# Switched attention: output products for the chosen experts only, through slots in DRAM

## The reference

```python
gate = (one_hot(top2(sigmoid(raw))) * vals / vals.sum()).sum(-2)       # [B, S, H, E], two of eight not zero
q, k = per head x @ q_w[h].T, x @ k_w[h].T
xv = jnp.einsum('bsd,hedp->bshep', x, v_w.reshape(H, E, D, P))
v = jnp.einsum('bshep,bshe->bhsp', xv, gate_v)
att = softmax(jnp.einsum('bhqp,bhkp->bhqk', q, k) * SCALE)
ctx = jnp.einsum('bhqk,bhkp->bqhp', att, v)
weighted = ctx[:, :, :, None, :] * gate_o[..., None]
out = jnp.einsum('bshep,hepd->bsd', weighted, o_w.reshape(H, E, P, D))
```

## Time and profile before

| | us |
|---|---|
| median of 3 runs | 2651.47 (2650.15 to 2653.01) |
| profiled execution: time, span | 2653.63, 2651.9 |
| TensorE busy | 2339.9 (88%) |
| VectorE busy | 1732.3 (65%) |
| ScalarE busy | 1372.8 (52%) |
| GpSimd busy | 539.1 (20%) |
| mean granted clock of TensorE | 0.951 |

### The profile page before, as it was taken

One profiled execution on the slowest core, in us unless ns is written; L12 is line 12 of the kernel. 1 busy time (PEld: TensorE's weight loads), 2 busy tenths in 40 slices (PEclk: granted clock), 3 DMA queues, 4 the chain that ended last, 5 costly groups with the idle time before them and its releaser, 6 DMA issues. The chain is left out here.

```text
span 2651.9 us, 51036 instructions
## 1 busy us (share of the span) xinstructions
PE 2339.9 (88%) x15539; PEld 1826.2 (69%) x15539; DVE 1732.3 (65%) x4474; ACT 1372.8 (52%) x3690; POOL 539.1 (20%) x639
## 2 busy tenths in 40 slices
PE   7679999859999958888699999589999999999995
PEld 5457777748999845555477777477777777777762
DVE  2346766755888656666367667546676776767677
ACT  2146666744666525555276667465444444444430
POOL 3000000010111230000100000054343343434321
PEclk9789999969999979999799999789999999999998
DMA  2065566323666410000455665010010100101000
GB/s 79 0 153 121 120 119 129 74 69 93 217 207 212 126 50 1 0 0 0 105 133 120 121 131 118 23 52 17 21 37 2 36 17 22 36 1 37 1 1 28
DMA packets 182198, 187.58 MB, mean 71 GB/s; under 512 B 55281, under 2 KB 173506, under 8 KB 182018
## 3 DMA queue, kind: packets, MB, share of 16 engines
q1 hardware_dynamic: 178466, 176.18, 26.7%
q0 software_dynamic: 3552, 9.18, 1.2%
HBM read 144.23 MB, written 41.09 MB: 70 GB/s over the span
## 5 line engine op out<-in xcount | busy, mean ns | idle before, releaser
L800 ACT ACTIVATE cross_pr<-cross_sc,cross_mn 112x375 f32<-112x375 f32 x512 | 310.4, 606 | 233.0 <-DVE cross_mn L890 232.1
L2385 ACT ACTIVATE switch_vt<-switch_ps,switch_chosen 112x128 f32<-112x128 f32 x1024 | 290.3, 368 | 266.2 <-PE switch_ps L106 255.8
L890 DVE CUSTOM_DVE_ANT_0 cross_sc<-cross_ps,cross_masked 112x375 f32<-112x375 f32 x512 | 273.3, 544 | 178.4 <-PE cross_ps L688 157.5
L2459 DVE SCALAR_TENSOR_TENSOR all_x<-switch_ps,switch_go,all_x 112x256 f32<-112x256 f32 x512 | 245.7, 480 | 217.7 <-PE switch_ps L106 212.2
L696 PE MATMUL cross_ps<-all_ident,cross_pr 112*125 112x112 f32 x1536 | 257.9, 277 | 22.9 <-DVE cross_pt L897 21.5
L696 PEld LDWEIGHTS cross_ps<-all_ident,cross_pr 112*125 112x125 f32 x1536 | 235.3, 191 | 44.5 <-DVE cross_pt L897 27.8
L2250 POOL TENSOR_TENSOR switch_v_halves<-switch_vt 112x512 f32<-112x512 f32 x128 | 164.6, 1286 | 482.6 <-ACT switch_vt L2385 482.4
L2459 DVE SCALAR_TENSOR_TENSOR switchgates_x_odd<-switch_ps,switch_go,switchgates_x_odd 112x256 f32<-112x256 f32 x512 | 243.5, 476 | 0.0
L688 PE MATMUL cross_ps<-cross_k,cross_q 96*112 96x376 f32 x512 | 222.9, 436 | 13.8 <-DMA cross_k<-cross_k_dram 10.7
L104 PE MATMUL switch_ps<-switch_ow,switch_cth 128*112 128x512 f32 x512 | 208.5, 407 | 11.9 <-DVE switchgates_x_odd L2459 11.5
L104 PE MATMUL switch_ps<-switch_vw,switchgates_xh 128*112 128x512 f32 x512 | 207.5, 405 | 7.9 <-DVE switch_vw L2444 7.9
(11 more groups left out here) (375 smaller groups left out, 5522.6 us busy)
## 6 DMA issues: line engine op xcount, KB each, us to landing
experts_w_raw<-in_L_ffn_w_dram SPq DMA_DIRECT2D x42, 1024.0 KB, 5.5
cross_k<-cross_k_dram SPq DMA_DIRECT2D x96, 375.0 KB, 8.0
cross_k_dram<-cross_ks SPq DMA_DIRECT2D x32, 750.0 KB, 4.5
cross_cx_raw<-in_ctx_dram SPq DMA_DIRECT2D x32, 375.0 KB
cross_q<-cross_q_dram SPq DMA_DIRECT2D x192, 56.0 KB, 4.4
switch_raw<-in_L_ffn_v_w_dram SPq DMA_DIRECT2D x16, 512.0 KB
switch_raw<-in_L_ffn_o_w_dram SPq DMA_DIRECT2D x8, 1024.0 KB, 5.5
cross_q_dram<-cross_qs SPq DMA_DIRECT2D x32, 224.0 KB, 3.4
```

Of the source, the lines that this page charges most:

```text
L800: nc.scalar.activation(pr[:, h % NB, :], sc[:, h % NB, :], ACT.Exp, bias=mn[parity][:, h:h + 1], scale=-1.0, accum_out=rs[parity][:, h:h + ...
L890: nc.vector.tensor_tensor_reduce(out=sc[:, h % NB, :], in0=ps[0:T, SCORES + h % 2, 0:S2], in1=mask_of[:], scale=-0.25, scalar=3e38, op0=AL ...
L2385: last = nc.scalar.activation(vt[:, b % 2, n * EH + e, :], ps[0:T, VALUES + n, e * PW:(e + 1) * PW], ACT.Copy, scale=chosen[parity][:, b, ...
L2459: nc.vector.scalar_tensor_tensor(out=total[:, b, :], in0=ps[0:T, OUTPUTS + n % 2, i * D:(i + 1) * D], scalar=go[:, b, e:e + 1], in1=total[ ...
```

## The change

The values of a head are still computed for all experts. The outputs are computed for the two chosen experts of each token alone. For each head VectorE now also counts the assignments and finds the slot of each (`prepare_head`, in place of `choose_gates`); TensorE sums the counts with two products (`count`). GpSimd scatters the context rows of each batch twice, once for each choice, into an array of 21 x 256 slots in DRAM. SP loads each tile of 256 slots back, and the weights of the tile's expert, whose number it reads from `owner`. TensorE transposes the tile and multiplies it in plain fp32, ScalarE copies both, and SP stores the product in a second array. GpSimd gathers two rows for each token, and VectorE adds them, times gate over softmax sum, to x. x_odd is gone. The split of the contexts and of the output weights is gone. Of the values, ScalarE scales experts 0 to 3 and VectorE adds 4 to 7; GpSimd's sums are VectorE's.

The tiles of head h stand between step 7 of period h+1 and step 7 of period h+2, behind the values of the heads h+1 and h+2; the gathers stand in steps 8 to 23 counted from the start of period h+2, the additions three steps later. The loop over heads is unrolled, and two periods and more follow the last head's values. Both slot arrays are filled with zeros once. In the diff HALVES is 32, TILE_SLOT 14, SB 2, RING (buffers of a tile) 3 and FETCH (buffers of a gather) 6; the functions in their order are the places of tiles and gathers, the load of a tile, the fill, the scatter and the gather, `turn` and `product`, and VectorE's values and combination.

```diff
+        def tile_half(g):
+            h, t = g // TILES, g % TILES
+            return HALVES * (h + 1) + TILE_SLOT + HALVES * t // TILES
+        def turn_half(g):
+            return tile_half(g) - 1 if g % TILES == 0 else tile_half(g - 1)
...
+            j = (p - 2) * B + b - B // 2
...
+            def load_tile(g):
+                h, t, i = g // TILES, g % TILES, g % RING
+                if t == 0:
+                    sp.wait_ge(owner_ready, h + 1)
+                    for n in range(2):
+                        sp.wait_ge(scattered[n], (h + 1) * 2 * CB * 2 * 16)
+                wait(sp, turned, g - RING + 1)
+                sp.dma_start(rows_in[i][:], slots_x[h % 2][t * ST:(t + 1) * ST].rearrange("(q p) d -> p q d", p=P))\
+                    .then_inc(rows_loaded[i], 16)
+                wait(sp, prod_done, g - RING + 1)
+                e = sp.value_load(owner[0:1, h, t:t + 1], min_val=h * E, max_val=h * E + E - 1)
+                sp.dma_start(ow[i][:].unsqueeze(1), o_w[ds(e, 1)].rearrange("a p d -> p a d")).then_inc(ow_loaded[i], 16)
...
+            sp.wait_ge(zero_ready, 1)
+            for i in range(2):
+                sp.dma_start(slots_x[i].rearrange("(n p) d -> p n d", p=P),
+                             zero[:].unsqueeze(1).broadcast_to([P, TILES * SB, PW])).then_inc(filled, 16)
             load_v(1)
...
-                pool.tensor_tensor(v_halves[:], vt[:, b % 2, 0:E // 2, :], vt[:, b % 2, E // 2:E, :], ALU.add)\
...
+                pool.wait_ge(ctx_ready, n + 1)
+                for j in range(CB):
+                    for k in range(2):
+                        at = bass.IndirectOffsetOnAxis(ap=slot[:, h, k, c * CB + j:c * CB + j + 1], axis=0)
+                        pool.indirect_dma_start(out=slots_x[h % 2], out_offset=at, in_=ctx[n % 2][:, j, :], in_offset=None)\
+                            .then_inc(scattered[n % 2], 16)
...
+                if b == 0:
+                    for n in range(RING):
+                        pool.wait_ge(y_stored[n], (h + 1) * TILES // RING * 16)
+                wait(pool, combined, j - FETCH + 1)
+                for k in range(2):
+                    at = bass.IndirectOffsetOnAxis(ap=slot[:, h, k, b:b + 1], axis=0)
+                    pool.indirect_dma_start(out=fetched[i][:, k, :], out_offset=None, in_=slots_y[h % 3], in_offset=at)\
+                        .then_inc(gathered[i], 16)
...
-                    split_product(nc, ps[0:T, OUTPUTS + n % 2, :], [a[:, b * T:(b + 1) * T] for a in (cth, ctl)],
-                                  [a[:, 2 * n:2 * n + 2, :].rearrange("p e d -> p (e d)") for a in ow[parity]])\
...
+                wait(pe, ct_ready, g)
+                for q in range(SB):
+                    last = nc.tensor.transpose(ps[:, TILE_X, q * P:(q + 1) * P], rows_in[g % RING][:, q, :], ident[:])
...
+                pe.wait_ge(ct_ready, g + 1)
+                pe.wait_ge(ow_loaded[g % RING], (g // RING + 1) * 16)
+                wait(pe, y_ready, g)
+                for q in range(SB):
+                    last = nc.tensor.matmul(ps[:, TILE_Y, q * D:(q + 1) * D], ct[g % 2][:, q * P:(q + 1) * P], ow[g % RING][:],
+                                            start=True, stop=True)
...
+                    for n in range(2):
+                        if p < HS:
+                            values(p, b, n)
+                        for g in tiles_at(tile_half, p, b, n):
+                            product(g)
+                        for g in tiles_at(turn_half, p, b, n):
+                            turn(g)
...
-                        nc.vector.scalar_tensor_tensor(out=total[:, b, :],
-                                                       in0=ps[0:T, OUTPUTS + n % 2, i * D:(i + 1) * D],
-                                                       scalar=go[:, b, e:e + 1], in1=total[:, b, :], op0=ALU.mult,
-                                                       op1=ALU.add).then_inc(out_step, 1)
...
+                for e in range(EH):
+                    part = vt[b % 2][:, e, :]
+                    last = nc.vector.scalar_tensor_tensor(out=part, in0=ps[0:T, VALUES + 1, e * PW:(e + 1) * PW],
+                                                          scalar=chosen[h % 2][:, b, EH + e:EH + e + 1], in1=part,
+                                                          op0=ALU.mult, op1=ALU.add)
+                last.then_inc(v_dve, 1)
+                dve.wait_ge(v_dve, slot + 1)
+                nc.vector.tensor_tensor(v_half[:], vt[b % 2][:, 0:EH // 2, :], vt[b % 2][:, EH // 2:EH, :], ALU.add)\
...
+                nc.vector.tensor_tensor(v[:, b, :], v_half[:, 0, :], v_half[:, 1, :], ALU.add).then_inc(v_ready, 1)
...
+                    nc.vector.scalar_tensor_tensor(out=x[:, b, :], in0=fetched[i][:, k, :], scalar=gts[:, h, k, b:b + 1],
+                                                   in1=x[:, b, :], op0=ALU.mult, op1=ALU.add)\
...
-                ch.link(nc.vector.tensor_add(x[:, part, :], x[:, part, :], x_odd[:, part, :]))
```

More of the change, by code:

```diff
@@ L2268, in _ @@
+            for p in range(PERIODS + 1):
+                for b in range(B):
+                    n = p * NC + (b - SCATTER_AT) // CB - 1
+                    if b % CB == SCATTER_AT and 0 <= n < HS * NC:
+                        scatter(n)
+                    j = fetched_at(p, b)
+                    if j is not None:
+                        fetch(j)
         @block.tensor
@@ L2316, in attend, with count @@
-            def attend(chunk, c, step):
+                wait(pe, (v_act, v_dve)[n], slot)
+                for k in range(DC):
+                    last = split_product(nc, ps[0:T, VALUES + n, :], [a[:, k, b * T:(b + 1) * T] for a in (xh, xl)],
+                                         [a[:, k, n * EH * PW:(n + 1) * EH * PW] for a in vw[h % 2]],
+                                         k == 0, k == DC - 1)
+                last.then_inc(values_done, 1)
+            def count(h):
+                pe.wait_ge(const_ready, 1)
+                pe.wait_ge(both_ready, h + 1)
+                wait(pe, qk_ready, ((h - 1) * NC + (COUNT_AT - 2) // CB) * 2 + 2)
+                rows_of = both[:].rearrange("p b e -> p (b e)")
+                nc.tensor.matmul(ps[0:T, COUNTS, 0:B * E], before[:], rows_of, start=True, stop=True)
+                nc.tensor.matmul(ps[0:T, COUNTS, B * E:2 * B * E], ones[:], rows_of, start=True, stop=True)\
+                    .then_inc(counted, 1)
@@ L2390, in attend @@
-            def attend(chunk, c, step):
+                    act.wait_ge(chosen_ready, h + 1)
+                wait(act, v_added, slot - 1)
+                act.wait_ge(values_done, slot * 2 + 1)
+                for e in range(EH):
+                    last = nc.scalar.activation(vt[b % 2][:, e, :], ps[0:T, VALUES, e * PW:(e + 1) * PW], ACT.Copy,
+                                                scale=chosen[h % 2][:, b, e:e + 1])
+                last.then_inc(v_act, 1)
+            def attend(n, step):
@@ L2424, in drain, with store_turned @@
[L2424 to L2429 removed]
+                else:
+                    act.wait_ge(c_done, n + 1)
+                    wait(act, scattered[n % 2], n // 2 * CB * 2 * 16)
+                    nc.scalar.copy(ctx[n % 2][:].rearrange("p a b -> p (a b)"), ps[0:T, TURNED, :]).then_inc(ctx_ready, 1)
+            def store_turned(g):
+                act.wait_ge(turned, g + 1)
+                wait(act, prod_done, g - 1)
+                nc.scalar.copy(ct[g % 2][:], ps[:, TILE_X, 0:ST]).then_inc(ct_ready, 1)
@@ L2514, in drain @@
[L2514 to L2527 removed]
+                    dve.wait_ge(ri_ready, n + 1)
```

545 lines of the change are left out of this document (306 added, 239 removed).

## The result

The changed kernel takes 2575.32 us (median of 4 runs, 2568.27 to 2578.28) against 2651.68 before, a ratio of 0.9708 with a 95% interval of 0.9688 to 0.9729. The forecast was 2587, so the sign, the range and the likeliest case hold. Four of the terms behind it were off by more than 4 us, in both directions, and they cancel in part: that the total is within 12 us is luck.

A forecast was written before the change was run, and what follows sets the result against it. TensorE's own work was taken to bound the period, GpSimd close behind. Start 1723.5, head 0 77, period 1 80, six periods 558, drain 129 and norm 20.4 gave span 2588, so 2587 us (2.4% faster); range 2540 to 2640.

The forecast's parts named there:

- the likeliest case: Switch stage: TensorE sets a period of 89 to 96 us, total 2555 to 2607 us; chance 0.54.
- Start, head 0, period 1: Switch stage's opening: start at 1723.5, head 0 77 us (2 for filling slots), period 1 with 12 tiles 80 us.
- The period: Six full periods of the switch stage: 93 us each, TensorE's 87.4 plus 5.6 of coupling.
- The floor: TensorE's own work in a period with tiles: 87.4 us, 63.9 without them.
- The stall: Tile copies queue behind ScalarE's activations; ct_ready comes 1.4 us late in four batches a period: 5.6 us added.
- Its rivals at 1.5 us and more: GpSimd's indirect DMAs: at 1.5 us or stretched they set the period, 2613 or 2640 (0.20); slower case 2721 (0.09).
- the port lock: VectorE and GpSimd share a port pair: some 15 small operations per head could each delay an indirect DMA; total 2640.
- the lockstep rival: VectorE's 76 us stand in fixed order between TensorE and ScalarE, each waiting: period 100, total 2629 us; chance 0.12.
- The drain: After the last values: tiles from 25, 52 for tiles, 5.5 store and landing, 43 gathers, 1.7 and 0.9; 129 summed.
- the likeliest error: In the drain: tiles at 3.5 us each in place of 2.5 would add 21 us.
- The floor rival: Period at 87.4 us and drain at 117, head 6's gathers holding GpSimd until 75: total 2536 us; chance 0.05.
- The final norm: After the drain: 25.3 before, less 4 x 1.23, gives 20.4 us.

## Why the prediction was right, and where its terms were off

**Start, head 0, period 1.** 1723.5 forecast and 1722.8 measured, 77 and 72.0, 80 and 79.8. The fill of the slots costs SyncE 9.3 us of issue and nothing that shows; the 2 us for it, and 3 of head 0's, were too much.

**The period**, 93 against 89.7, six times: the largest error, 20 us. The floor was right: 87.4 forecast, and TensorE is busy 86.7 us of a period without gathers and 87.3 with them. The stall was mis-sized: 5.6 forecast, 2.3 by the waits for copied tiles and 2.4 by TensorE's idle time. I had taken every first batch of a chunk to lose 1.4 us, but it happens 11 times in six periods, not 24.

**VectorE** has 69.9 us of work in a full period where 76 was forecast, ScalarE 47.4 where 51 was.

**GpSimd**, 64 x 1.34 = 86 forecast, 82 in the kernel, and 79.8 to 82.6 where it is the bound. Its rivals at 1.5 us and more are refuted. The stretching they built on is real, but it needs a scatter that starts beside a weight split: at most 2 of a period's 64, about 1 us each, and not 15. Of the port lock that the Trainium skill's page "SBUF — State Buffer", section "Who interferes with whom", tells for copies, casts and tensor_scalar, the switch stage shows no cost: the 69 transfers that overlap such an operation take 0.95 us on average and 1.19 at most. Against the lockstep rival stands the run without gathers: 15 us less on VectorE and half of GpSimd's work move the period by 1.5.

**The drain**, 129 against 136. (The forecast's own terms add to 128; its sum took 129.) Head 7's rows load at 24.3 (25). Then 21 tiles take 65 us from the first turn, where 52 was forecast: the step is 3.03, not 2.5, since the product runs at the low clock, 2.07. The text had named this as the likeliest error, at 3.5. Store 2.9 (5.5), gathers 39 (43), landing and last combination 2.7. The floor rival's first term was right: head 6's gathers hold GpSimd for 75.7 us (75), so faster tiles alone can't bring the drain under some 117. The forecast also has 117 there, but by luck: its own 75, 43, 1.7 and 0.9 make 121.

**The final norm**, 20.4 against 25.1: taking off the x_odd adds was right, but a stage end soon after indirect transfers has a gap of 5.8 us where before it was 0.95. No row used for the term showed that; the end of `stage_experts` in the same trace did.

**Balance.** Values end 25.6 us earlier than forecast, the drain is 7 and the norm 4.7 longer: 14 of span. The mechanism (TensorE's own work sets the period, a chain that nothing covers sets the drain) held; the closeness of the total came of errors that cancel.

## What to carry to other kernels

When a dense product is traded for sorted slots, the steady state gains the product's time and the last head pays the whole chain: scatter, tiles, store, gather. Here 146 us are saved up to the last value (2559 to 2413), 8 to 11 of them the loop's, and 69 are given back in the drain (67 to 136). Compute the last unit the old way, where nothing follows to cover the chain (30 us here), and look at what then sets the drain before doing more. In a drain where TensorE waits on copies, price its products at the low clock: idle products bought 7.5 us by the traces, 12.5 by the ratios.

## What the runs showed of the hardware

- An indirect transfer of 112 rows costs GpSimd 0.92 to 1.0 us and 0.30 to the next; 103 in a row took 1.23 each. VectorE being busy 77% of the time adds little (0.97 on average). The exception is a scatter that starts during VectorE's subtraction of 128x1024 with two inputs in SBUF (1.22 us): ten of these took 1.65 to 2.06 us and ended 0.8 behind the subtraction.
- A stage whose last GpSimd work is a gather ends 8.5 us behind it (5.8 behind VectorE in the changed kernel). `stage_experts`, with its last gather 9 us before GpSimd's last operation, still has 7.1 us behind that operation. Within a stage the next instruction follows at once.
- A loop end in the kernel before costs about 3 us of the period.
- The same work ahead of the switch stage took 1708.4 to 1716.4 us from profile to profile, so one profile can't tell 5 us of the whole.
- One program whose steady state is the same, instruction for instruction, as another's took 140 to 145 us a period in place of 90 to 91, in both of its runs: the updates of its semaphore `s_done` come up to 15 us behind the products they report, where the other's come 0.01 behind. What delays them is open.
